# Two transformer layers on one core: a query's product moved ahead of a maximum's, its rest to the head of VectorE's step, eight target slots, and two kinds of transfer issued by other engines

## The reference

```python
def reference(...):                    # x: 8 samples x 512 tokens x 128
    xn = _layernorm(x)
    x = x + _L0_attn_ref(xn, ...) + _L0_ffn_ref(xn, ...)   # causal attention without softmax; FP4-rounded FFN
    xn = _layernorm(x)
    x = x + _L1_attn_ref(xn, ...) + _L1_ffn_ref(xn, ...)
    return x

def _L1_attn_ref(x, ...):              # 16 query heads of 64, one key and one value head
    scores = einsum("bshd,btd->bhst", q, k) / sqrt(64)
    w = softmax(scores, axis=-1)
    return einsum("bhst,btd->bshd", w, v).reshape(B, S, 1024) @ Wo + bo

def _L1_ffn_ref(x, ...):               # 8 experts, each token goes to its best 2
    selected = top-2 gates, divided by their sum
    h = gelu(x @ W1[e] + b1[e]);  out = sum over e of selected[e] * (h @ W2[e] + b2[e])
```

## Time and profile before

| | before |
|---|---|
| median of 3 runs | 1462.54 us (1460.64 to 1464.70) |
| profiled execution, its own time | 1460.9 us |
| its span, first to last instruction | 1459.0 us |
| mean granted clock of TensorE | 0.953 of full speed |

### The profile page before, as it was taken

One profiled execution on the slowest core, in us unless ns is written; L12 is line 12 of the kernel. 1 busy time (PEld: TensorE's weight loads), 2 busy tenths in 40 slices (PEclk: granted clock), 3 DMA queues, 4 the chain that ended last, 5 costly groups with the idle time before them and its releaser, 6 DMA issues.

```text
span 1459.0 us, 22233 instructions
## 1 busy us (share of the span) xinstructions
PE 1300.1 (89%) x7377; PEld 767.7 (53%) x7377; DVE 1013.9 (69%) x2393; ACT 708.1 (49%) x1300; POOL 252.5 (17%) x306
## 2 busy tenths in 40 slices
PE   4569888999999999999999999999998778979877
PEld 2335445555555555555555555555454466656634
DVE  7777776578757875787677767776776456666655
ACT  3136454544454445444545454545454464757531
POOL 3132222201010111011001200110002035242510
PEclk9579999999999999999999999999999899999989
DMA  2042442002000200020002000200003255445242
GB/s 72 14 130 93 128 139 103 31 17 77 24 29 17 82 22 26 17 82 24 24 17 82 26 23 17 82 27 21 16 18 113 78 167 171 135 157 163 72 154 59
DMA packets 72372, 100.26 MB, mean 69 GB/s; under 512 B 29196, under 2 KB 49228, under 8 KB 68292
## 3 DMA queue, kind: packets, MB, share of 16 engines
q1 hardware_dynamic: 59876, 70.69, 15.6%
q0 software_dynamic: 10192, 27.44, 5.8%
q10 hardware_dynamic: 2192, 0.71, 0.2%
HBM read 59.86 MB, written 38.68 MB: 68 GB/s over the span
## 4 chain that ended last, share of the span: by engine, by line
PE 61%; DVE 15%; issue 12%; POOL 6%; DMA 2%; SPq 2%; ACT 1%; DVEq 0%; POOLq 0%; ACTq 0%
PE bank L1423 13%; PE bank L1395 7%; PE bank L1351 6%; PE bank L1396 6%; PE bank L1434 6%; POOL y_rows L701 5%; PE bank L1455 4%; DVE mneg L990 3%; PE bank L1275 3%; PE bank L1259 3%; PE bank L1260 2%; PE bank L1261 2%; PE bank L1310 2%; DVE q_lm L984 2%; PE bank L1292 1%
## 5 line engine op out<-in xcount | busy, mean ns | idle before, releaser
L821 ACT ACTIVATE wide<-bank 128x512 f32<-128x512 f32 x512 | 301.5, 604 | 502.8 <-PE bank L1396 492.5
L990 DVE TENSOR_REDUCE mneg<-bank 128x1 f32<-128x512 f32 x512 | 347.4, 686 | 203.6 <-PE bank L1351 197.7
L1395 PE MATMUL bank<-q_hh,k_hl 128*128 128x512 f32 x512 | 236.2, 461 | 19.8 <-DMA q_lm<-mrow 18.2
L1423 PE MATMUL bank<-wide,v_w 128*32 128x512 f32 x2048 | 248.7, 604 | 0.5 <-issue 0.5
L1351 PE MATMUL bank<-k_hl,q_hh 128*128 128x512 f32 x512 | 208.5, 409 | 36.0 <-DVE mneg L990 22.1
L1396 PE MATMUL bank<-q_lm,k_h 65*128 65x512 f32 x512 | 204.2, 399 | 0.0
L1395 PEld LDWEIGHTS bank<-q_hh,k_hl 128*128 128x128 f32 x512 | 97.7, 191 | 151.6 <-issue 109.4
L1351 PEld LDWEIGHTS bank<-k_hl,q_hh 128*128 128x128 f32 x512 | 98.7, 193 | 73.7 <-issue 52.8
L631 POOL TENSOR_TENSOR rs<-rs,power 128x4 f32<-128x4 f32 x24 | 24.6, 1026 | 626.2 <-DVE rs L892 626.2
L1434 PE MATMUL bank<-wide,ones 128*32 128x512 f32 x992 | 129.1, 592 | 0.0
L701 POOL DMA_INDIRECT y_rows<-y_m,to_u x92 | 92.4, 1004 | 177.0 <-DVE y_m L1117 155.0
(11 more groups left out here) (230 smaller groups left out, 2001.4 us busy)
## 6 DMA issues: line engine op xcount, KB each, us to landing
w_t<-w_rows SPq DMA_DIRECT2D x23, 1024.0 KB
x_rows<-part_h POOLq DMA_DIRECT2D x65, 258.0 KB, 5.7
inv<-inverse_scratch SPq DMA_DIRECT2D x124, 128.0 KB, 3.0
w_rows<-w_t SPq DMA_DIRECT2D x8, 1024.0 KB, 4.9
x_m<-x_rows SPq DMA_DIRECT2D x23, 258.0 KB
stage<-in_L_ffn_W SPq DMA_DIRECT2D x16, 256.0 KB, 4.8
yab<-y_rows SPq DMA_DIRECT2D x8, 512.0 KB, 7.3
xin<-in_L_attn_x SPq DMA_DIRECT2D x8, 256.0 KB, 4.0
```

The costliest lines, as they stand in the source:

```text
L821: act.activation(wide[:, st.g % WIDE, :], ps, ACT.Exp, scale=SCALE1).then_inc(wide_full, 1)
L990: dve.tensor_reduce(mneg[:, (gh // 2) % 2, col:col + 1], ps[:], X, ALU.max, negate=True)\
L1395: pe.matmul(ps, k_hl[:, n, t], q_hh[:, gh % HEADS, :], start=True, stop=False)
L1423: pe.matmul(ps_out[0][rows, :], v_w[:, n, c, TILE * d:TILE * d + TILE], weights, start=(c == 0), stop=(c == TT - 1))
```

## The change

The change has five parts. (1) At k % 4 == 1 PE makes the query before the maximum's product and the turn of the maxima, where it came last. (2) At k % 4 == 2 DVE makes the query's rest before the first layer's cut of that step, where it came behind it. (3) `to_u` and its semaphores have TO = 8 slots, where they had WT = 4; a tile's rows are turned and split in its step 0 and its result in step 2, where both were in step 1. (4) `store_m` is issued by ACT, at the end of the head's events of the same step, where SP issued it. (5) The first weights are loaded at k = 1, 5, 10 and 13 and the first rows at k = 10, and the results are read back by POOL behind its last scatter.

```diff
-    WT, XT, YT, YM = 4, 2, 2, 3
+    WT, XT, YT, YM, TO = 4, 2, 2, 3, 8
...
-    LANDED_AT = 41
+    ROWS_AT, WEIGHTS_AT = 10, [1, 5, 10, 13]
...
     def tile_events(st):
-        if st.g is None or st.g % TT != 1:
+        if st.g is None:
             return []
-        here = st.g // TT
-        return [(use, tile_of[i]) for use, i in (("tx", here + 1), ("ty", here - 2)) if i in tile_of]
+        here, c = divmod(st.g, TT)
+        use, i = {0: ("tx", here + 1), 2: ("ty", here - 2)}.get(c, (None, None))
+        return [(use, tile_of[i])] if i in tile_of else []
...
         ahead_ = gh + LEAD + s // TT
+        if s % TT == 1 and 0 <= ahead_ + 1 < H * NB:
+            events.append(("q", ahead_ + 1))
         if 0 <= ahead_ < H * NB:
             events.append(("mx", ahead_, s % TT))
         if s == TT + 1 and 0 <= gh + 2 < H * NB:
             events.append(("mt", (gh + 2) // 2))
-        if s % TT == 1 and 0 <= ahead_ + 1 < H * NB:
-            events.append(("q", ahead_ + 1))
...
-                        for t in range(WT):
-                            load_tile_weights(t)
-                    if st.kind == "o" and st.k == 9:
+                    if st.kind == "o" and st.k in WEIGHTS_AT:
+                        load_tile_weights(WEIGHTS_AT.index(st.k))
+                    if st.kind == "o" and st.k == ROWS_AT:
                         for t in range(XT):
                             load_tile_rows(t)
...
+            for t in range(TILES - TO, TILES):
+                landed(pool, t)
+            for n in range(NB):
+                pool.dma_start(yab[:, n], y_rows[1 + 2 * S * n:1 + 2 * S * (n + 1), :]
+                               .rearrange("(i p b) d -> p i b d", p=P, b=2)).then_inc(yab_loaded[n], 16)
...
+            def store_m(pair):
+                read_out(act, ("mt", pair))
+                at_ = (2 * pair) % HEADS
+                act.dma_start(q_lm[DK:DK + 1, at_:at_ + 2, :].bitcast(F32), mrow[:, pair % 2, :].bitcast(F32))\
+                   .then_inc(m_loaded[pair % 2], 16)
...
-                if t >= WT:
-                    landed(dve, t - WT)
+                if t >= TO:
+                    landed(dve, t - TO)
...
             for st in steps:
+                if split_head(st) is not None:
+                    lo_q(split_head(st))
                 if st.kind in ("pre", "o"):
                     for n, k in ((st.r + 1, st.k), (st.r + 2, st.k - ATT)):
                         for _ in range(L0_DVE.count(k) if 0 < n < NB else 0):
                             next(cuts[n], None)
-                if split_head(st) is not None:
-                    lo_q(split_head(st))
```

More of the change, by code:

```diff
@@ L374, in two_layers @@
         b_t = sb("b_t", [P, WT, 8])
-        to_f, to_u = sb("to_f", [P, TT]), sb("to_u", [P, WT, TT], U32)
+        to_f, to_u = sb("to_f", [P, TT]), sb("to_u", [P, TO, TT], U32)
         zeros = part_h[:].rearrange("p n s -> p (n s)")[:, 0:TT * ROW].bitcast(F32)
@@ L406, in two_layers @@
         xm_loaded = [sem(f"xm_loaded{i}") for i in range(XT)]
-        to_set, y_scattered = sem("to_set"), [sem(f"y_scattered{i}") for i in range(WT)]
+        to_set, y_scattered = sem("to_set"), [sem(f"y_scattered{i}") for i in range(TO)]
         yab_loaded = [sem(f"yab_loaded{i}") for i in range(NB)]
@@ L548, in load_tile_rows @@
                   .then_inc(xm_loaded[t % XT], 16)
-            def load_landed(n):
-                if n == 0:
-                    for t in range(TILES - WT, TILES):
-                        landed(sp, t)
-                sp.dma_start(yab[:, n], y_rows[1 + 2 * S * n:1 + 2 * S * (n + 1), :]
-                             .rearrange("(i p b) d -> p i b d", p=P, b=2)).then_inc(yab_loaded[n], 16)
             def store_out(n):
@@ L564, in _ @@
             for st in steps:
-                for event in head_events(st):
-                    if event[0] == "mt":
-                        store_m(event[1])
                 for r, k in row_steps(st):
@@ L700, in _ @@
                 for i in range(TT):
-                    pool.indirect_dma_start(y_rows, bass.IndirectOffsetOnAxis(ap=to_u[:, t % WT, i:i + 1], axis=0),
-                                            y_m[:, t % YM, i, :], None).then_inc(y_scattered[t % WT], 16)
+                    pool.indirect_dma_start(y_rows, bass.IndirectOffsetOnAxis(ap=to_u[:, t % TO, i:i + 1], axis=0),
+                                            y_m[:, t % YM, i, :], None).then_inc(y_scattered[t % TO], 16)
+            for t in range(TILES - TO, TILES):
[3 more added lines that the diff above has]
+                               .rearrange("(i p b) d -> p i b d", p=P, b=2)).then_inc(yab_loaded[n], 16)
         @block.scalar
@@ L832, in _ @@
                         copy_m(event[1])
+                for event in head_events(st):
+                    if event[0] == "mt":
+                        store_m(event[1])
                 for _, n, s in l0_events(st):
@@ L1106, in tile_in @@
                 dve.tensor_tensor(xt_l[:, i, :], ps[:], xt_h[:, i, :].bitcast(F32), ALU.subtract).then_inc(free, 1)
[L1107 to L1108 removed]
+                if t >= TO:
+                    landed(dve, t - TO)
                 target = x_m[:, t % XT, :, P]
                 link(dve.scalar_tensor_tensor(to_f[:], target, 0.0, spare[:, t, :], ALU.is_equal, ALU.mult))
[L1111 removed]
+                dve.tensor_tensor(to_u[:, t % TO, :], to_f[:], target, ALU.add).then_inc(to_set, 1)
             def tile_turned(t):
```

10 lines of the change are left out of this document (1 added, 9 removed).

## The result

The changed kernel takes **1414.58 us** (median, 1412.93 to 1415.41) against 1461.59 (1458.53 to 1464.7) for the kernel before on the same chip: ratio 0.9677, interval 0.9654 to 0.97. The profiled execution took 1414.91 us with a span of 1413.0. The forecast of 1413.5 was 1.1 us off. That it came so near is in part luck: of its four terms one had the wrong sign, one was nearly twice what was found and two were too small, and these errors cancel.

What follows compares the result with a forecast made beforehand. PE's work was taken to bound each row, with the winnable waits in the last row. Gains of 4 + 4.5 + 34 + 6.5 = 49 us from 1460.9 gave 1411.9, as median 1413.5; range 1394 to 1431.

Steps and rivals of the forecast that it cites:

- What bounds the kernel: PE's work bounds second-layer rows; the last row's waits, 46 us, outweigh all waits of the seven other rows.
- B: Start of the last row: the late maxima behind four weight loads go, a wait for rows comes; gain 4.5 us.
- C: Tiles of the last row: eight slots remove the waits for `part_l` and half clocks; gain 34 us.
- D: End of the last row: maxima no longer wait behind the results' loads; gain 6.5 us.
- the two groups: Last row's PE waits: 28.2 us for `part_l` and 18.2 us for two late transfers of the maxima.
- A: Steps of every row: query first on PE, its rest first on DVE; gain 4 us.
- sum per row, seven rows: Gains and losses at k = 44, 62, 59 and 33 give 0.6 us per row, 4 us over seven rows.
- ACT's added work at nothing: 64 store issues on ACT at k % 8 == 5 cost nothing; 45 us if their cover were gone.
- The slower one: Rival: the store of the maxima lands too late in every pair; 1484 us at a 4.5 us landing, chance 0.04.
- The tiles' wait moves: Rival: DVE's copy to `y_m` or `part_l` becomes late, half of C stays; 1430.5 us, chance 0.08.
- B and D come to nothing: Rival: weights and `yab` only swap one late transfer for another; 1424.5 us, chance 0.15.
- The row order pays more: Rival: each row's half clock goes and the first rows are in time; 1394.5 us, chance 0.12.

Runs made afterwards that it cites:

- a0: The changed kernel itself, measured again beside later runs, with nothing altered: 1416.2 us, ratio 0.9692 to the kernel before.
- e9: Changed kernel with the last row's first rows loaded at k = 5 and weights at k = 1, 10, 11, 13: 1411.6 us, ratio 0.9591 to the kernel before.
- b1: Kernel before with eight target slots and their semaphores alone, nothing else of the change: 1420.8 us, ratio 0.9718 to the kernel before.
- e4: Changed kernel with four target slots again in place of eight, all else kept: 1468.4 us, ratio 1.0047 to the kernel before.
- e6: Changed kernel with the store of the maxima issued by SP again, all else kept: 1420.4 us, ratio 0.971 to the kernel before.
- e8: Changed kernel with all four loads of weights at k = 0 and the rows at k = 9: 1425.7 us, ratio 0.9688 to the kernel before.
- e7: Changed kernel with the results read back by SP at k = 41, the store staying on ACT: 1420.0 us, ratio 0.9707 to the kernel before.

## Why the prediction came out, step by step

**What bounds the kernel** held: the waits of the last row decided, which by the marks gave 48.4 us (B, C and D), all that stands ahead of them a loss of 2.5. The reading that the 46 us of the two groups outweigh all waits of the seven other rows was a little too strong: PE's waits from 110 to 1119 us of the kernel before come to 47.6, and 16.7 of them stand before 262, in row 0, which the prediction passed over.

**A, the row order: wrong in sign.** Predicted a gain of 4, found a loss of 2.5 in the profiled execution. Mean over the six executions of the same head, the loss is 1123.6 - 0.7 - 1121.8 = 1.1, against the two with the head of before, 1121.27 and 1122.30. Both numbers also hold whatever the store's move to ACT gives there. The step that failed is "sum per row, seven rows". The regular rows had the right sign: 0.6 predicted, and as the mean of four rows 0.4 in the profiled execution (143.59 to 143.17) and 0.2 in a0 and e9 (143.42). But row 0 and the steps ahead of it were left out of the sum, and there the changed kernel loses: by the ninth turn 4.3 us (257.69 - 252.69 - 0.7; 1.7 in a0), of which the rows behind win back 1.8 (0.8 in a0). It also lumped two edits: the rest first gives 7.4 by itself, and the query ahead takes 10.0. I had gone through the waits of a row, and asked of each only whether the query's bank is free by then; I had not asked what else waits while the query goes first. At k = 33 the wait is 1.27, not 2.0, so the loss of 0.7 that I put there did not come; the waits of 0.34 at 508.28 and of 0.76 at 524.93, which I had not foreseen, came instead, and at k = 59 three waits of together 1.9 stand where two of 1.9 stood.

**ACT's added work at nothing** held in the sense that it costs nothing that these runs can show; whether the move itself gives something ahead of the last row stays open (1.2 us within a group, up to 4.0 across).

**B**: predicted 4.5, found 2.4. The terms that it removes held, 11.35 us and a half clock. The term that was mis-sized is the wait for the rows, 9.24 against 7.3, and with it the half clock, 10.2 us long. SP reached the rows about 12 us after k = 8 in place of 10.2: the four loads of `inv`, which stand ahead of them in both kernels, were issued from 1135.51 on, 5.9 us after k = 8, and before from 1142.12 on, 4.2 after it. Why SP was later there no run isolates. Then came the weights at 1139.25.

**C**: predicted 34, found 37.9. The mechanism is the slots' (b1), as argued. The size lies above the upper bound of 37. I had allowed 3 us for waits that take their place, and one came, of 2.08; and the half clocks were worth 10.8 rather than 9, as PE's own work between the first and the last `y_t` went from 182.5 us to 171.7. What the text says of the steps ("evens it out") is not borne out: without the slots they cost (e4), and no gain shows with them (b1).

**D**: predicted 6.5, found 8.1. The landing was 4.70 where I took 2.5, so PE waited 0.96; the turn at k = 53 waited 0.58 where I took 2. POOL issued the loads at 1359.98 in 0.8 us each, inside the bounds of 0.55 and 2.2. The two costs that the text names, about 1 and 2, make 3.0 and not 3.2.

**The sum.** Against what the marks give, the terms are off by -6.5 (A), -2.1 (B), +3.9 (C) and +1.6 (D), together -3.1 of 49. The medians differ by 47.0, and the kernel before took 0.9 us less beside the changed one than the forecast started from. That errors of 1.6 to 6.5 us cancel to 1.1 is luck; what was right is that the waits of the last row pay for the change, C above all.

**The rivals.** The slower one did not occur: PE waits 2.9 us for the maxima in all, twice, once in row 0 beside loads of stages. "The tiles' wait moves" did not occur. "B and D come to nothing" is half right for B. "The row order pays more" is the opposite of what it did. Of what the profile was to show, four points missed: the wait at k = 33 near 2.0, the one of `x_m` of 5 to 9 us (9.24), no wait for the maxima above 1 us (1.95 in row 0), and the wait at k = 62, which is not gone but 0.65 us long, behind ACT's `qk`, as part A itself had it.

## What to carry to other kernels

When an edit reorders a step, cost each of its parts by itself and also in the stretches where the pattern is disturbed (the first row, its loads), since a gain per regular row can be lost there. Ask of a resource that is taken earlier what it is kept from, not only what it is free of. When a ring of slots is reused too early, more slots are the cheap test: one number here brought nine tenths of the whole change. And in a list with several calls of one helper, find out which call an instruction of the trace is before moving it.

## What was not expected of the hardware

A store of 4 KB is slow beside megabytes on another queue. From issue to PE's use it took, with the mean busy share of the DMA engines in that stretch (of the packets that start in it, so it can pass 1). In each row PE was waiting for the store when it landed:

| store | us | DMA share |
|---|---|---|
| e6, k = 8, the last load of weights issued 6.6 us earlier | 1.96 | 0.09 |
| before, | 1.98 | 0.09 |
| e6, store on SP, `yab` from POOL | 4.14 | 0.72 |
| changed kernel, store on ACT, `yab` from POOL | 4.70 | 0.72 |
| the same place in a0 | 4.68 | 0.85 |
| the same place in e8 | 5.40 | 0.95 |
| changed kernel, row 0 (166.01 to 171.44), beside the stage loads | 5.43 | 0.86 |
| e8, beside three loads of weights from SP | 5.88 | 0.94 |
| e7, `yab` from SP | 5.43 | 1.03 |
| before, behind `yab` on its own queue | 5.71 | 1.06 |

With the engines idle it is 2 us, and with them 72% busy or more 4.1 to 5.9, longer in the main the busier they are; which queue the store is on hardly shows. So the other queue helped because the store was issued sooner, no longer 8.4 us behind the first of SP's loads as in the earlier trace rows, and at most by a little because it landed faster. The Trainium skill, "DMA: Bandwidth & Descriptors", section "Queues, rings and completion order", lets a completion count land only after all earlier writes of that engine, in every queue; the numbers beside traffic agree with it. They would also agree with the engines' bandwidth being shared, and no run here separates the two.
